# Scale and bias of the experts' norm: from the first weights of stage one to the turned rows of stage two

## What is computed

```python
h = _layernorm(x, axis=-1) * (1 + cb) + sb            # hidden_states
for e in range(E):                                     # E = 8, top 2 by a router
    h = _layernorm(hidden_states, ln_g[e], ln_b[e])    # scale and bias of expert e
    h = gelu(einsum('bld,di->bli', h, w1[e]) + b1[e])  # D = 256 -> I = 1024
    h = einsum('bli,id->bld', h, w2[e]) + b2[e]        # I = 1024 -> D = 256
    out = out + combine[..., e:e + 1] * h
```

## Time and profile before

| | us |
|---|---|
| three runs | 1335.91, 1337.92, 1338.38 |
| the profiled execution | 1338.33 |
| its span, first to last instruction | 1336.6 |
| outside the span | 1.7 |
| stage one and set-up | 433 |
| bridge | 33 |
| stage two (71 tiles) | 778 |
| stage three | 93 |

### The profile page before, as it was taken

One profiled execution on the slowest core, in us unless ns is written; L12 is line 12 of the kernel. 1 busy time (PEld: TensorE's weight loads), 2 busy tenths in 40 slices (PEclk: granted clock), 3 DMA queues, 4 the chain that ended last, 5 costly groups with the idle time before them and its releaser, 6 DMA issues.

```text
span 1336.6 us, 29653 instructions
## 1 busy us (share of the span) xinstructions
PE 1119.8 (84%) x8406; PEld 888.2 (66%) x8406; DVE 937.7 (70%) x2983; ACT 572.9 (43%) x1162; POOL 391.0 (29%) x343
## 2 busy tenths in 40 slices
PE   5888988888954099999999999999999999999200
PEld 1344555454534089999999999999999999999100
DVE  5478888888874366666666666666666666666598
ACT  2566667666732043333333333343333333333332
POOL 1112546455656311111111111111111111111365
PEclk8789778878865599999999999999999999999655
DMA  5444454635432546532234522522222212432697
GB/s 164 131 151 131 158 188 145 212 144 197 129 122 75 210 169 190 189 115 60 60 94 150 166 83 61 190 67 62 60 60 60 60 60 60 140 105 68 201 352 263
DMA packets 104742, 177.03 MB, mean 132 GB/s; under 512 B 21933, under 2 KB 75305, under 8 KB 98569
## 3 DMA queue, kind: packets, MB, share of 16 engines
q1 hardware_dynamic: 91752, 141.04, 34.0%
q0 software_dynamic: 12960, 35.67, 7.2%
HBM read 228.63 MB, written 63.38 MB: 218 GB/s over the span
## 4 chain that ended last, share of the span: by engine, by line
PE 64%; DVE 13%; issue 7%; POOL 4%; DMA 2%; SPq 1%; DVEq 1%; ACT 1%; POOLq 0%; ACTq 0%
PE bank L1215 28%; PE bank L1227 28%; DVE wbuf L1034 3%; DVE st L675 2%; PE bank L1204 2%; PE bank L1118 2%; POOL lists L470 2%; POOL rs L463 2%; PE bank L1180 1%; PE bank L1189 1%; DVE rowbuf L792 1%; DVE rowbuf L794 1%; DVE resid L852 1%; DVE mv L680 1%; DMA lists<-nrm,slot 1%
## 5 line engine op out<-in xcount | busy, mean ns | idle before, releaser
L1215 PE MATMUL bank<-nh,wbuf 128*128 128x256 bf16 x2272 | 466.3, 273 | 2.1 <-DVE nl L975 1.5
L634 ACT ACTIVATE gf<-bank,b1t 128x256 f32<-128x256 f32 x568 | 268.8, 473 | 376.4 <-PE bank L1215 371.3
L1227 PE MATMUL bank<-wbuf,gh 128*128 128x256 bf16 x2272 | 402.8, 273 | 0.0
L496 POOL DMA_INDIRECT y_rows<-rowbuf,ydst x142 | 136.6, 962 | 661.8 <-DVE rowbuf L998 638.2
L1006 DVE CAST gh<-gf 128x256 bf16<-128x256 f32 x568 | 165.6, 292 | 226.9 <-ACT gf L634 199.8
L1215 PE MATMUL bank<-nl,wbuf 128*128 128x256 bf16 x1136 | 310.4, 273 | 0.0
L1227 PE MATMUL bank<-wbuf,gl 128*128 128x256 bf16 x1136 | 309.6, 273 | 0.0
L1008 DVE TENSOR_TENSOR gl<-gf,gh 128x256 bf16<-128x256 f32 x568 | 241.6, 425 | 19.5
L1215 PEld LDWEIGHTS bank<-nh,wbuf 128*128 128x128 bf16 x2272 | 222.8, 98 | 28.4 <-DVE nl L975 1.9
L1227 PEld LDWEIGHTS bank<-wbuf,gh 128*128 128x128 bf16 x2272 | 222.2, 98 | 26.0 <-DVE gl L1008 0.3
L470 POOL DMA_INDIRECT lists<-nrm,slot x128 | 147.6, 1153 | 133.8 <-DVE slot L925 89.6
(11 more groups left out here) (178 smaller groups left out, 1217.7 us busy)
## 6 DMA issues: line engine op xcount, KB each, us to landing
wbuf<-wsplit SPq DMA_DIRECT2D x142, 1024.0 KB
rowbuf<-lists SPq DMA_DIRECT2D x71, 260.0 KB, 2.7
wbuf<-in_L_ffn_w SPq DMA_DIRECT2D x16, 1024.0 KB, 6.9
wsplit<-wbuf SPq DMA_DIRECT2D x16, 1024.0 KB, 7.2
wbuf<-y_rows SPq DMA_DIRECT2D x32, 512.0 KB, 6.0
b2t<-in_L_ffn_b SPq DMA_DIRECT2D x71, 128.0 KB
resid<-in_L_attn_x SPq DMA_DIRECT2D x16, 512.0 KB
out<-resid SPq DMA_DIRECT2D x16, 512.0 KB, 4.2
```

What stands on the lines that cost most here:

```text
L496: g.indirect_dma_start(y_d, bass.IndirectOffsetOnAxis(ap=ydst[:, r, h:h + 1], axis=0), yt[:, r, h, :], None).then_inc(y_out[r], 16)
L634: a.activation(gf[:, c % 2, :], MM[c % 2][:, 0:TOK], ACT.Gelu, bias=b1t[:, r, c:c + 1]).then_inc(gf_s, 1)
L1215: last = t.matmul(MM[c % 2][:, 0:TOK], w, m[:, r, k, :], start=n == 0, stop=n == 5)
L1227: last = t.matmul(ACC[r][h][:, 0:D], g[:, c % 4, h * P:(h + 1) * P], w, start=c == 0 and n == 0, stop=c == NI - 1 and n == 2)
```

## The change

The scale and bias no longer touch the weights. A small table `evec` (b1, ln_g and ln_b of each expert, 12 numbers for each partition) is written once to unused rows of `y_rows`, and the 12 columns of a tile's expert are loaded with the tile in place of `b1t`. In stage two ACT applies ln_g and ln_b to each half of the turned rows, twice: once into bf16 (`nh`) and once into f32 (`nf`); DVE takes `nf` less `nh`.

```diff
@@ SP, stage one @@
+                if isinstance(i, int) and i == 1:
+                    sp.wait_ge(evec_s, 3)
+                    sp.dma_start(y_d[2 * NTOK:2 * NTOK + E * P, 0:NI + 4].rearrange("(e p) i -> p e i", p=P), evec[:, :, :]).then_inc(evec_out, 16)
...
-                    sp.wait_ge(b1p_s, half + 1)
                     if not isinstance(half, int) or half + 1 < E:
                         load_w1(half + 1)
-                    sp.wait_ge(b1r_s, half + 1)
-                    for n in range(2):
-                        sp.dma_start(b1r_d[half, n:n + 1, :] if isinstance(half, int) else b1r_d[ds(half, 1), n, :], b1row[n]).then_inc(b1_out, 16)
@@ SP, bridge @@
-            sp.wait_ge(b1_out, 32 * E)
-            sp.dma_start(vrow[0:E * NI, :], b1r_d.rearrange("e n (i p) -> (e n i) p", p=P)).then_inc(got_b1v, 16)
-            sp.wait_ge(b1f_s, 1)
-            sp.dma_start(b1f_d.rearrange("e p i -> p e i"), b1f[:, :, :]).then_inc(b1_out, 16)
@@ SP, tile loads @@
-                sp.dma_start(b1t[:, r, :], b1f_d[ds(e, 1)]).then_inc(got_b1[r], 16)
+                sp.dma_start(evt[:, r, :], y_d[ds(e * P + 2 * NTOK, P), 0:NI + 4]).then_inc(got_ev[r], 16)
@@ ACT, stage one @@
-                if project and r == 1:
-                    act.wait_ge(b1p_s, half + 1)
-                    wait_past(act, b1_out, 32 * half)
-                    hold(act, "act")
-                    a.activation(b1row[0], Q[0:1, :], ACT.Copy)
-                    a.activation(b1row[1], V[0:1, :], ACT.Copy).then_inc(b1r_s, 1)
...
-                    for k in range(NK):
-                        a.activation(wbuf[:, 0, k * 1024:(k + 1) * 1024], w1f[:, k, :], ACT.Copy,
-                                     scale=lge[:, k:k + 1]).then_inc(head1_s, 1)
+                    a.activation(wbuf[:, 0, 0:2048], w1f.rearrange("p k i -> p (k i)"), ACT.Copy).then_inc(head1_s, 1)
@@ ACT, stage two @@
-            def head_rows(j, r):
-                act.wait_ge(tr_s, j + 1)
-                wait_past(act, mm1_s, NI * (j - 1))
-                a.activation(nh[:, r, :, :].rearrange("p k n -> p (k n)"), TR[r][:, :], ACT.Copy).then_inc(nh_s, 1)
+            def head_rows(j, half, r, k):
+                if k == 0:
+                    act.wait_ge(tr_s, j + 1)
+                    act.wait_ge(got_ev[r], 16 * half + 16)
+                    wait_past(act, mm1_s, NI * (j - 1))
+                    wait_past(act, nl_s, j)
+                    hold(act, "act")
+                g, b = evt[:, r, NI + k:NI + k + 1], evt[:, r, NI + 2 + k:NI + 3 + k]
+                a.activation(nh[:, r, k, :], TR[r][:, k * TOK:(k + 1) * TOK], ACT.Identity, bias=b, scale=g).then_inc(nh_s, 1)
+                a.activation(nf[:, k, :], TR[r][:, k * TOK:(k + 1) * TOK], ACT.Identity, bias=b, scale=g).then_inc(nf_s, 1)
...
-                    if c == 5 and not last_tile:
-                        head_rows(j + 1, 1 - r)
+                    if c in (5, 6) and not last_tile:
+                        head_rows(j + 1, half + r, 1 - r, c - 5)
@@ DVE, stage one @@
-                    for k in range(NK):
-                        v.scalar_tensor_tensor(wbuf[:, 0, 2048 + k * 1024:2048 + (k + 1) * 1024], w1f[:, k, :], lge[:, k:k + 1],
-                                               wbuf[:, 0, k * 1024:(k + 1) * 1024], ALU.mult, ALU.subtract).then_inc(rest1_s, 1)
+                    v.tensor_tensor(wbuf[:, 0, 2048:4096], w1f.rearrange("p k i -> p (k i)"), wbuf[:, 0, 0:2048], ALU.subtract).then_inc(rest1_s, 1)
...
-                    v.tensor_copy(lge[:, :], lngb[:, half + 1, :] if isinstance(half, int) else lngb[:, ds(half + 1, 1), :]).then_inc(lge_s, 1)
@@ DVE, bridge and stage two @@
-            dve.wait_ge(b1v_ps, 1)
-            v.tensor_tensor(b1f[:, :, :].rearrange("p e i -> p (e i)"), vecs[:, VEC_B1:VEC_G], V[:, 0:E * NI], ALU.add).then_inc(b1f_s, 1)
...
-                dve.wait_ge(nh_s, j + 1)
-                v.tensor_tensor(nl[:, r, :, :], TR[r][:, :].rearrange("p (k n) -> p k n", k=NK),
-                                nh[:, r, :, :], ALU.subtract).then_inc(nl_s, 1)
+                dve.wait_ge(nf_s, NK * j + NK)
+                v.tensor_tensor(nl[:, r, :, :], nf[:, :, :], nh[:, r, :, :], ALU.subtract).then_inc(nl_s, 1)
...
                     if c == 5 and not last_tile:
+                        destinations(j + 1, half + r, 1 - r)
+                    if c == 6 and not last_tile:
                         split_rows(j + 1, half + r, 1 - r)
-                    if c == 7 and not last_tile:
-                        destinations(j + 1, half + r, 1 - r)
@@ PE, stage one @@
-                    for n, row in enumerate((Q, V)):
-                        for k in range(NK):
-                            last = t.matmul(row[0:1, :], lge[:, 2 + k:3 + k], w1f[:, k, n * 512:(n + 1) * 512], start=k == 0, stop=k == NK - 1)
-                    last.then_inc(b1p_s, 1)
@@ PE, stage two @@
-                    if c == 4 and not is_last:
+                    if c == 3 and not is_last:
                         turn(j + 1, half + r, 1 - r)
```

More of the change, by code:

```diff
@@ L140, in adaln_moe_kernel @@
         gl = sb("gl", [P, 4, TOK], bf16)
-        b1t = sb("b1t", [P, 2, NI])
+        evt = sb("evt", [P, 2, NI + 4])
         b2t = sb("b2t", [P, 2, D])
@@ L856, in step @@
                     choose(i - 4, r)
-                if project and r == 1 and not (isinstance(i, int) and i == NB - 1):
-                    dve.wait_ge(rest1_s, NK * half + NK)
-                    dve.wait_ge(b1p_s, half + 1)
-                    hold(dve, "dve")
-                    v.tensor_copy(lge[:, :], lngb[:, half + 1, :] if isinstance(half, int) else lngb[:, ds(half + 1, 1), :]).then_inc(lge_s, 1)
             def cols(t, b):
```

47 lines of the change are left out of this document (17 added, 30 removed).

## The result

The changed kernel takes 1422.26 us in the median of 4 runs (1421.44 to 1428.87), the kernel before 1337.72 beside it (1335.91 to 1338.38): a ratio of 1.0651, 95% interval 1.0618 to 1.0684. That is 84.5 us more. The forecast was 1399.6, 62 us more, with a range to 1420: the direction, the place and the mechanism came as forecast, the size fell 2 us outside the range. The profiled execution has a span of 1421.2 us at a mean granted clock of 0.879.

A forecast was written before the change was run, and what follows sets the result against it. PE was taken to bound stage two, 778 us of the 1336.6 us span. The sum was 1338.3 - 1.0 (stage one) - 1.65 (bridge) + 1.4 (first tile) + 63 (`y_out` wait) = 1400; 1399.6 against the median, range 1354 to 1420.

The forecast's parts named there:

- the margin of 0.65 us: Stage two, kernel before: `nl` is done 0.65 us before the next tile starts; the change must not use that up.
- ACT in stage two: Stage two: four ACT operations of 0.57 us replace one copy and just fit; block 6's gelu stays at +9.15; 1.4 us once.
- Rival (c): Stage two: ACT falls behind as well and the scatter is 0.4 us later than read; 28 us more, 1427; chance 0.16.
- The wait for `y_out`: Stage two, DVE: row numbers wait for the scatter ahead of `nl`; 0.74 us late in 55 tiles, 1.59 in 14, 63 us.
- the next tile then starts 2.1 us after `y_out`: Stage two: row numbers 0.69, block 6 0.76, `nl` 0.68, signal 0.05, less about 0.1 for overlaps, follow the scatter's landing.
- its signal to PE 0.05: Stage two: the handover from the end of DVE's `nl` to PE was put at 0.05 us.
- Rival (a): Stage two: the scatter lands early enough, so 69 tiles lose only 0.30 us each, 21 us in all, 1358; chance 0.12.
- Stage one and bridge: Before stage two: stage one 1.0 us shorter in all, between -3 and +7, and the bridge 1.65 us shorter.
- The saving of 1.65 us in the bridge: Bridge: the round trip through `b1_rows`, PE and DVE goes, so SP's eight paddings start 1.65 us earlier.
- of 1.6 us on DVE: Stage one: DVE has less work for each of 8 experts; half of 8 x 0.4 us is counted as saved.
- the worry in that paragraph: Stage one: taking products out may lower PE's clock in odd steps; 7 of them may cost up to 1.0 us each.
- the 0.6 us taken for it: Stage one: net cost counted for PE's slower clock, 0.6 us, leaving 1.0 us saved in stage one.

The follow-up runs named there:

- (1): Changed kernel with DVE's old stage-two order: `nl` behind block 5, row numbers with their `y_out` wait behind block 7; 1343.16 us, ratio 1.0011 to the kernel before.
- (9): The kernel before, unchanged, run and profiled once more; ratio 0.9994 to itself.
- (2): Changed kernel with only the last row-number operation, the sum needing `y_out`, moved with its wait behind block 7; `nl` stays behind block 6; 1372.16 us, ratio 1.0212.
- (4): Changed kernel with `nl` behind block 5 and the row numbers, with their `y_out` wait, directly after it; 1350.39 us, ratio 1.0058 to the kernel before.
- 3: Kernel before with only the new stage-two order: row numbers behind block 5, `nl` behind block 6, transposes behind block 3; 1432.15 us, ratio 1.0668.
- 5: Changed kernel with DVE's b2 addition behind block 2 instead of block 1, so the scatter starts about 1.3 us later; 1528.16 us, ratio 1.1448.
- Experiment 13: Changed kernel with only PE's waits reordered: `nl` is waited for last, behind the two long-met waits; 1415.48 us, ratio 1.0610 to the kernel before.
- nl first: Changed kernel with `nl` behind block 5 and the row numbers behind block 7; ratios 1.0011 and 1.0012 to the kernel before in two measurements.
- 7: nl first plus four added products (8 records) on the w1 tile in each odd step of stage one; 1335.85 us, ratio 1.0011.
- 15: nl first with four added products on the w1 tile in each odd step of stage one, side by side without them; 1335.74 us, ratio 1.0013.
- 14: nl first once more, without added products, beside the version with them and the kernel before; 1335.15 us, ratio 1.0012.

## Why the prediction was right, and where it fell short

**What bounds the kernel; the margin of 0.65 us.** Right: with `nl` back behind block 5 the tile is 10.92 us again (1). But 0.65 us was the margin of one profile. In the second one of the same kernel (9) ACT's copy follows the transposes at once, at +7.19 (the tile from 705.06) and not at +7.91, and `nl` is done 1.21 us before the next tile starts at 715.98:

```profile
712.25 0.60 ACT L625 ACTIVATE nh<-bank 128x512 bf16<-128x512 f32 x1 [0.62 <-PE bank L1204]
...
714.08 0.68 DVE L975 TENSOR_TENSOR nl<-bank,nh 128x512 bf16<-128x512 f32 x1
```

**ACT in stage two.** Right to 0.02 us at every step of the tile shown. The operations take 557 and 563 ns (forecast 570) and the gelu of block 6 starts at +9.16; in (1), (2) and (4) it starts at +9.28, as said at (2) and (9). Rival (c), ACT behind too and a later scatter, did not come about, although its 1427 lies nearer to the result than the forecast does: by experiment 1 ACT's work costs nothing that can be measured, and the scatter did not land later.

**The wait for `y_out`.** Right in kind, and shown by experiments 1, 3, 4 and 5. The landing was forecast at +9.55 in plain tiles and +10.4 in those with weights. Worked out over the last 66 tiles it is +9.47 in 51 of them and +10.20 in 15. That is 0.08 us less than forecast in the mean, 5 us less in all. In the first three tiles with the wait it came at +11.5, +11.5 and +10.6, which is 4 us more. So the landing was not what was mis-sized.

**The step that failed: "the next tile then starts 2.1 us after `y_out`".** It is 2.46 us in the mean, 0.36 more, and 69 x 0.36 is 25 us. That is the miss: 63 + 25 - 5 + 4 is 87, and the windows show 87.0. (Not in this sum, and nearly cancelling: the very first tile, which has no such wait, took 13.08 us and not 12.08, and a tile of the kernel before is 10.92 us where 10.91 was reckoned with.) Two of its terms were too small. From the landing to the end of the row numbers I had 0.69 us, the operations alone, and nothing for the time from the landing to the first of them; it is 0.92 (landing 721.5, end 722.4). In the two tiles with the wait that are written out ahead of the loops the first of them starts 0.12 us after the landing, in the loops 0.23 to 0.24. And "its signal to PE 0.05" is what the first tile of the stage shows, which is written out as well; in the loops it is 0.13 and 0.24 by turns, 0.19 in the mean. Experiment 13 gives the cause of the second, and some 7 us of the loss back. For the first, the same handling of register values on DVE's side is an argument, not shown: the trace has a register operation of 46 ns at 721.6 between landing and row numbers, and no experiment moved it. The 1.34 us between (block 6 and `nl`) came as forecast.

```profile
L961 DVEq FUSED_REGOPS  x1: 46/46/46, 721.6 to 721.6; - x1
```

**Rival (a), 0.30 us a tile without any wait.** It is 0.43 in (2), 27 us and not 21. PE's signal is short by the same 0.14 us; but (2) also has one operation fewer ahead of `nl` and a gelu of block 6 that comes 0.13 us later. For the changed kernel's own queue the estimate at (2) is 0.34 us, 24 us.

**Stage one and bridge.** Forecast 2.65 us less, of which 1.4 is given back by the first tile: 1.25 less in all. Measured, by the timed ratios of nl first, 0.1% more, with 0 and 0.26% within the intervals. The saving of 1.65 us in the bridge and of 1.6 us on DVE cannot be seen beside the 2 to 3 us by which stage one's end moves and the 5 us of the paddings. The granted clock of the first 433 us fell from 0.81 to 0.75, as the worry in that paragraph had it, yet raising it again with added products (7, 15) gains nothing. No run shows the 0.6 us taken for it by themselves; its bound of +7 was not reached. The windows of two steps, from which I read a price of 1.0 us for the clock, differ in more than the clock; they are the earlier trace rows, and "rows 10" in that paragraph is a slip.

## What to carry to other kernels

Before an operation that everybody waits for is moved behind another in an engine's queue, ask what that other one waits for: the cost is not the length of the work in front but the time at which its last wait ends, here the landing of a scatter that had a whole tile of cover before. Put the operand that opens the next tile ahead of any wait for an old transfer; the same wait directly behind it cost a tenth as much. And read the price of a handover inside the loop, not in the tiles written out ahead of it, and place the wait that will end last behind the ones that are long met.

## What the runs showed of the hardware

Waits in a loop that compare with a register's value take time after the last real one has ended: the first product came 0.13 and 0.24 us by turns after its operand with two such waits behind the real one, 0.06 with them ahead of it (13). Eight paddings issued by one and the same program on SP took 14.9 us in one profile (1) and 9.1 in another (14); over all profiles it was 8.9 to 15.0. After PE had been idle for 2.0 to 2.4 us, 15 tiles of (5) ran their first 3.6 us at a granted clock of 0.53 to 0.57, 1.65 us lost on top of the idle time, and 45 did not; idle times of 0.3 to 1.7 us, as in the changed kernel, left the clock at 1.00 each time. And a granted clock of 0.75 or 0.80 over the 433 us of stage one, made by leaving out or adding 4.4 us of products in every other step, made no difference in time beyond the 0.15% to which each was measured (14, 15: 1.0012 and 1.0013).
